# Gathers of a two-layer graph kernel: buffers awaited per group of four, indices copied three batches ahead

## The chip, the cores and the metric

One Trainium2 chip, one of its cores. The time is that of the device in microseconds (us), from start to end of the program; the kernel before took 14879.7 us (median of 3 runs, 14873.69 to 14883.93). TensorE, VectorE, ScalarE and GpSimd are called PE, DVE, ACT and POOL, as the profile does; SP is SyncE, which only issues DMAs here. Each engine has a sequencer that reads its instruction stream in order, carries out waits and register operations itself and hands the rest to the engine.

## The reference, cut to what matters

6250 nodes of 128 float32, 206250 edges sorted by destination, 64 edge types.

```python
# layer 0 (L0)
msg = edge_weight[:, None] * x[src];  agg = segment_sum(msg, dst, N)
x = layernorm(x + (relu((x + agg) @ W1 + b1) @ W2 + b2))
# layer 1: three hops over the same edges; head = src, tail = dst
agg = x
for _ in range(3):
    h, t = agg[head], agg[tail]
    att = sum((h @ q_w) * tanh(rel * t @ k_w), axis=1)      # rel = edge_emb[edge_type]
    w = softmax of att over the edges of one head
    agg = normalise(segment_sum(w[:, None] * rel * t, head) / count)
    out = out + agg + x
x = layernorm(x + out)
```

Both layers read one row of 512 bytes for every edge, from an address that the data give: `x[src]` in L0, `agg[tail]` in each hop.

## The kernel before, in words

Edges are laid out in tiles of 128 (one per partition), 1664 tiles in all, so that the edges of one tile belong to one section of 128 nodes. Four tiles make a group (`GROUP`), and there are 416 groups (`z.slot_groups`). L0 goes once over the groups, each of the three hops once more: 1664 turns over a group, and 6656 gathers of 128 rows (64 KB).

Every engine runs its own software pipeline over the groups. A step `s` with number `i` holds the engine's share of several groups: `s.live(3)` is the work on group `i - 3`. `pipeline` (L125, for the hops) runs the first steps written out, then a hardware loop with `unroll` steps in its body, then the last ones written out. `phases` (L146, for L0) does this in blocks of 32 steps: twice `unroll` steps written out, then a loop for the rest. L0 also carries the second sort of the edges (its own matmuls, one-hots and DMAs) in the same steps.

In a hop, the chain of one group is: SP loads its `rel`, `mask` and four `window` tiles; POOL gathers its four `tails` tiles; ACT copies `rel` to PSUM (L1857); DVE multiplies it with the gathered rows into `rt` (L1771) and counts `s_rt` up; PE transposes `rt` (L1833, "rtt"); ACT copies that out (L1853); PE multiplies with `k_w` (L1829, "kw"); ACT takes tanh of it (L1849, `right`); PE forms the attention (L1818); DVE masks it (L1759); ACT takes the exponential (L1866, `weight`); PE transposes it (L1825), ACT copies that out (L1846, `weight_t`), PE sums the messages (L1838, "acc"), and DVE adds them to the section's sums (L1753). A step of ACT has the order `weight_t`, `right`, (index copy), rtt, `rel`, `weight`, `fade`. So each group passes from PE to ACT or DVE five times, each time by a semaphore.

In L0, ACT multiplies the gathered rows with the edge weights (L1394) and counts `s_rt` up, and PE sums them with one-hot matrices (L1406).

The gathers are issued by `pool_rows` (L616), the same for L0 and the hops. It works in batches of two groups (`BATCH`, eight gathers). The ring of row buffers holds four groups (`RING`), that of indices two batches. For each batch in the loop POOL's sequencer waits (L632 to L634) until both groups that had the buffers are used up (`freed` counts `s_rt` by 2) and until the batch's indices are copied (`copied`), then hands over eight indirect DMAs, then does its register additions (L636, L637) and waits for the next. The indices are copied by ACT out of the edge table (`scalar_idx`, L645 and L649): in step `i`, for even `i`, after the rows of group `i - 1` are used up, it copies those of groups `i + 2` and `i + 3`. The first two batches (16 gathers) are handed over at the start of a stage.

Of the kernel before, what the change touches and what calls it, by code (L numbers as in the profile page):

```python
# [15 lines left out]
P = 128  # L16
# [4 lines left out]
RING = 4  # L21
BATCH = 2
# [144 lines left out]
def gnn_two_layers(nc, x, src, dst, edge_type, edge_weight, w1, b1, w2, b2, edge_emb, q_w, k_w, out):  # L167
# [3 lines left out]
    with top:  # L171
# [492 lines left out]
        with ExitStack() as ctx:  # L664
# [60 lines left out]
            others = tensor(ctx, "l0_others", [P, z.slot_tiles + BATCH * GROUP], I32)  # L725
# [302 lines left out]
            idx = tensor(inner, "l0_idx", [P, 2, BATCH * GROUP], I32)  # L1028
# [385 lines left out]
            with nc.Block() as block:  # L1414
# [10 lines left out]
                def _(e):  # L1425
                    first_idx(e, others, idx)
                    phases(e, "ga", scalar_l0, z.slot_groups, steps, (UNROLL, 16 * GROUP))

                @block.vector
                def _(e):  # L1430
# [4 lines left out]
                    phases(e, "gv", vector_l0, z.slot_groups, steps, (UNROLL, GROUP * UNROLL))  # L1435
# [3 lines left out]
                def _(e):  # L1439
                    phases(e, "gt", tensor_l0, z.slot_groups, steps, (UNROLL, GROUP * UNROLL))  # L1440
            inner.close()
            s_copy_idx.base += z.slot_groups // BATCH + 1
# [92 lines left out]
        others = tensor(top, "tails_of_slots", [P, z.slot_tiles + BATCH * GROUP], I32)  # L1535
# [160 lines left out]
        for hop in range(HOPS):  # L1696
            with ExitStack() as ctx:
                qt = tensor(ctx, f"qt{hop}", [P, z.NP])
                idx = tensor(ctx, f"idx{hop}", [P, 2, BATCH * GROUP], I32)
# [44 lines left out]
                def vector_hop(s):  # L1744
# [21 lines left out]
                    if s.live(1):  # L1766
                        g4, g8 = s.slot(1, UNROLL), s.slot(1, UNROLL)
# [184 lines left out]
                with nc.Block() as block:  # L1952
                    @block.sync
                    def _(e):
                        e.wait_ge(s_qt.h, s_qt.at(node_groups))
                        pipeline(e, f"hs{hop}", sync_hop, z.slot_groups, deep, (UNROLL,) if first else (UNROLL, GROUP * UNROLL))
# [14 lines left out]
                    def _(e):  # L1971
                        vector_q(e)
                        pipeline(e, f"hd{hop}", vector_hop, z.slot_groups, deep, (UNROLL, 2 * UNROLL, GROUP * UNROLL, 16 * GROUP, 32))
# [3 lines left out]
                    def _(e):  # L1977
                        tensor_q(e)
                        pipeline(e, f"he{hop}", tensor_hop, z.slot_groups, deep, (UNROLL, GROUP * UNROLL, 16 * GROUP))

                    @block.scalar
                    def _(e):
                        first_idx(e, others, idx)
                        scalar_q(e)
                        pipeline(e, f"ha{hop}", scalar_hop, z.slot_groups, deep, (UNROLL, GROUP * UNROLL, 32))
                        scalar_nodes(e)
                s_copy_idx.base += z.slot_groups // BATCH + 1
# [62 lines left out]
```

## Time and profile before

| | |
|---|---|
| median of 3 runs | 14879.7 us |
| span of the profiled execution, first to last instruction | 14895.7 us |
| the three runs' times | 14873.69, 14879.7, 14883.93 us |
| PE busy | 9009.4 us (60%) |
| DVE, ACT busy | 6224.1 us (42%), 6149.7 us (41%) |
| POOL busy | 6417.6 us (43%) |
| granted TensorE clock, mean | 0.725 |
| L0 (gathers from 160.5 to 3251.3 us) | 1664 gathers |
| hops (gathers from 3532.0 to 14810.8 us) | 4992 gathers |

The profiled execution has no time of its own beside its span; the span is 16 us above the median of the runs. "Busy" of POOL is the time in which descriptors of a gather were written, not the transfer. A row "[6.54 <-ACT idx L649]" says that the engine sat idle for 6.54 us before this instruction and that what ended the idle time was ACT's instruction of line 649; "issue" is time for which the profile shows no wait, "remote" a semaphore event that it can put down to no instruction that had just ended. POOLq and DVEq are the sequencers' own instructions. The starts of PE's rows are recorded, their ends are modelled.

### The profile page before, as it was taken

The numbers are of one execution on the slowest core, as the hardware profiler recorded it, in microseconds if no ns is written. First come the engines' busy times: TensorE is split into PE (matmuls) and PEld (weight loads), VectorE is DVE, ScalarE is ACT, GpSimd is POOL, SyncE is SP. The second block draws the span as 40 slices with busy tenths as digits, with TensorE's granted clock in tenths as the row PEclk, the third lists the DMA queues.
The fourth block names the chain that finished last, engine by engine and source line by source line (L and its number), as shares of the span: only waits on it lengthen the run. The fifth ranks groups of instructions, "written<-read, shape, count | busy, mean of one in ns | idle before, by whom it ended". The sixth has DMA issues, their size and how long they took to land. (4 is left out here: it accounts for less than half of the span.)

```text
span 14895.7 us, 251017 instructions
## 1 busy us (share of the span) xinstructions
PE 9009.4 (60%) x47197; PEld 6806.5 (46%) x47197; DVE 6224.1 (42%) x27880; ACT 6149.7 (41%) x15788; POOL 6417.6 (43%) x6756
## 2 busy tenths in 40 slices
PE   2465555566777777777755555555555556555665
PEld 2343443444555555555544444444444444444444
DVE  3555555565333333333343333333334333333334
ACT  1355555553333333333334444444443444444443
POOL 4554554442444434444334444444434444444443
PEclk7566666667777777777777777777777777777777
DMA  2111111112444444444433333333343333333333
GB/s 63 37 37 34 36 35 35 33 35 77 127 125 126 125 125 126 125 125 126 124 102 105 106 104 106 104 105 101 108 99 105 104 104 107 102 105 105 109 109 93
DMA packets 1390477, 1399.81 MB, mean 94 GB/s; under 512 B 239512, under 2 KB 1066681, under 8 KB 1390137
## 3 DMA queue, kind: packets, MB, share of 16 engines
q1 hardware_dynamic: 1173398, 951.42, 21.2%
q0 software_dynamic: 216064, 444.28, 12.3%
q10 hardware_dynamic: 876, 2.56, 0.1%
q8 instruction: 51, 0.84, 0.0%
q14 instruction: 88, 0.71, 0.0%
HBM read 888.87 MB, written 183.76 MB: 72 GB/s over the span
## 5 line engine op out<-in xcount | busy, mean ns | idle before, releaser
L621 POOL DMA_INDIRECT tails<-node_rows,idx x4992 | 4732.3, 948 | 6564.6 <-ACT idx L649 5017.2
L1753 DVE SCALAR_TENSOR_TENSOR acc<-acc,fade,banks 128x129 f32 x4992 | 1718.4, 344 | 5486.8 <-remote 3164.9
L1838 PE MATMUL banks<-rt,weight_t 128*128 128x129 f32 x9984 | 1783.3, 335 | 1486.3 <-issue 802.1
L1838 PEld LDWEIGHTS banks<-rt,weight_t 128*128 128x128 f32 x9984 | 1607.8, 244 | 1631.4 <-issue 1206.6
L621 POOL DMA_INDIRECT l_rows<-in_x_dram,l_idx x1664 | 1585.1, 953 | 1529.5 <-ACT l_idx L649 1017.3
L1846 ACT ACTIVATE weight_t<-banks 128x512 f32<-128x512 f32 x1248 | 745.5, 597 | 3569.1 <-remote 2286.4
L1825 PE MATMUL banks<-ident,weight 128*128 128x128 f32 x4992 | 1070.4, 353 | 1878.0 <-ACT weight L1866 1767.1
L1818 PE MATMUL banks<-right,window 128*128 128x128 f32 x9984 | 1774.8, 335 | 459.9 <-issue 459.2
L1818 PEld LDWEIGHTS banks<-right,window 128*128 128x128 f32 x9984 | 1590.2, 242 | 538.2 <-issue 510.7
L1829 PE MATMUL banks<-rtt,k_sb 128*128 128x512 f32 x2496 | 1741.3, 789 | 1.4 <-ACT rtt L1853 1.4
L1825 PEld LDWEIGHTS banks<-ident,weight 128*128 128x128 f32 x4992 | 752.0, 181 | 2041.5 <-ACT weight L1866 1931.4
L1759 DVE CUSTOM_DVE_ANT_0 att<-banks,mask 128x128 f32<-128x128 f32 x4992 | 1236.7, 285 | 888.7 <-remote 574.4
L1866 ACT ACTIVATE weight<-att,low 128x128 f32<-128x128 f32 x4992 | 1583.4, 395 | 1.7 <-DVE low L1789 1.5
L1853 ACT ACTIVATE rtt<-banks 128x512 f32<-128x512 f32 x1248 | 743.4, 596 | 1597.2 <-remote 1447.3
L1849 ACT ACTIVATE right<-banks 128x512 f32<-128x512 f32 x1248 | 744.4, 596 | 1535.2 <-remote 798.3
L1833 PEld LDWEIGHTS banks<-ident,rt 128*128 128x128 f32 x4992 | 781.9, 172 | 1247.7 <-issue 894.1
L1771 DVE TENSOR_TENSOR rt<-banks,tails 128x512 f32<-128x512 f32 x1248 | 857.9, 687 | 547.2 <-remote 180.2
L1833 PE MATMUL banks<-ident,rt 128*128 128x128 f32 x4992 | 937.3, 321 | 241.5 <-DVE rt L1771 237.0
L1239 ACT ACTIVATE apart<-spread,spot_left 128x256 f32<-128x256 f32 x1534 | 655.2, 495 | 1030.0 <-remote 761.9
L1406 PE MATMUL banks<-l_weighed,l_hot 128*128 128x128 f32 x3328 | 756.5, 395 | 428.2 <-DVE acc L1371 217.7
L1406 PEld LDWEIGHTS banks<-l_weighed,l_hot 128*128 128x128 f32 x3328 | 649.6, 289 | 559.2 <-issue 549.1
L1394 ACT ACTIVATE l_weighed<-l_rows,l_weights 128x128 f32<-128x128 f32 x1664 | 526.8, 387 | 546.1 <-remote 394.4
(309 smaller groups left out, 9792.2 us busy)
## 6 DMA issues: line engine op xcount, KB each, us to landing
window<-qt SPq DMA_DIRECT2D x4992, 64.0 KB
rel<-rel_kept SPq DMA_DIRECT2D x832, 256.0 KB
rows_in<-tile_rows SPq DMA_DIRECT2D x416, 256.0 KB
rel_kept<-rel SPq DMA_DIRECT2D x416, 256.0 KB
mask<-mask_kept SPq DMA_DIRECT2D x832, 128.0 KB
tails<-node_rows,idx POOLq DMA_INDIRECT x4992
mask_kept<-mask SPq DMA_DIRECT2D x416, 128.0 KB
l_rows<-in_x_dram,l_idx POOLq DMA_INDIRECT x1664
```

The lines of the kernel that those rows point to most:

```text
L621: e.indirect_dma_start(out=rows[:, g, t % GROUP, :], out_offset=None, in_=of, in_offset=bass.IndirectOffsetOnAxis(ap=idx[:, b, t:t + 1], a ...
L1406: mm = s.e.matmul(bank[g2][:, t * P:t * P + P], hot[:, g2, t, :], weighed[:, g2, t, :], start=True, stop=True)
L1753: e.scalar_tensor_tensor(to, to, fade[:, g2, t:t + 1], bank[b_acc + t // 2][:, t % 2 * WIDE:t % 2 * WIDE + WIDE], ALU.mult, ALU.add).then_ ...
L1759: e.tensor_tensor_reduce(att[:, g2, t, :], bank[b_att][:, t * P:t * P + P], mask[:, g4, t, :], 1.0, START, ALU.add, ALU.min, tile_low[:, g ...
L1771: e.tensor_tensor(rt[:, g4, :, 0:z.D], of, tails[:, g8, :, :], ALU.mult).then_inc(s_rt.h, 1)
L1818: mm = e.matmul(bank[b_att][:, t * P:t * P + P], window[:, g4, t, :], right[:, g2, t * P:t * P + P], start=True, stop=True)
L1825: mm = e.transpose(bank[b_et][:, t * P:t * P + P], weight[:, g2, t, :], ident[:, :])
L1829: e.matmul(bank[b_kw][:, :], k_sb[:, :], rtt[:, s.slot(2, 2), :], start=True, stop=True).then_inc(s_kw.h, 1)
L1833: mm = e.transpose(bank[b_rtt][:, t * P:t * P + P], rt[:, s.slot(1, UNROLL), t, 0:z.D], ident[:, :])
L1838: mm = e.matmul(bank[b_acc + t // 2][:, t % 2 * WIDE:t % 2 * WIDE + WIDE], weight_t[:, s.slot(4, 2), t, :], rt[:, s.slot(4, UNROLL), t, :] ...
L1846: e.activation(weight_t[:, s.slot(4, 2), :, :].rearrange("p t d -> p (t d)"), bank[b_et][:, :], ACT.Copy).then_inc(s_ets.h, 1)
L1866: e.activation(weight[:, g2, t, :], att[:, g2, t, :], ACT.Exp, scale=-1.0, bias=low[:, g4, t + 1:t + 2]).then_inc(s_exp.h, 1)
```

## The change

The ring of row buffers keeps its four groups, but POOL now waits for each group by itself: before the four gathers of group g it waits until group g - 4 is used up, hands over four gathers, adds 1 to `freed`, and goes to the next group. The ring of indices grows from two batches to four (`HELD` = 8 groups). `first_idx` copies four batches ahead of the loop, and in step `i` ACT copies the indices of groups `i + 6` and `i + 7` where it copied those of `i + 2` and `i + 3`, with the same wait (group `i - 1` used up); POOL waits for a batch's indices once per two groups. The loops over the groups of all engines go over eight steps (`TURN`) where they went over four, with the rates of their counters doubled: in `pipeline` 51 turns a hop where there were 102, in `phases` 16 steps written out and two turns of eight where there were 8 and six of four.

```diff
+HELD = 8
+TURN = 8
@@ pool_rows
-            def batch(b):
-                for t in range(BATCH * GROUP):
-                    g = b * BATCH + t // GROUP
-                    e.indirect_dma_start(out=rows[:, g, t % GROUP, :], out_offset=None, in_=of,
-                                         in_offset=bass.IndirectOffsetOnAxis(ap=idx[:, b, t:t + 1], axis=0)).then_inc(sp_tail[g].h, 16)
-
-            for b in range(2):
-                e.wait_ge(s_copy_idx.h, s_copy_idx.at(b + 1))
-                batch(b)
+            def gather(g):
+                b, first = g // BATCH % (HELD // BATCH), g % BATCH * GROUP
+                for t in range(GROUP):
+                    e.indirect_dma_start(out=rows[:, g % RING, t, :], out_offset=None, in_=of,
+                                         in_offset=bass.IndirectOffsetOnAxis(ap=idx[:, b, first + t:first + t + 1], axis=0)).then_inc(sp_tail[g % RING].h, 16)
+
+            for g in range(RING):
+                if g % BATCH == 0:
+                    e.wait_ge(s_copy_idx.h, s_copy_idx.at(g // BATCH + 1))
+                gather(g)
...
-            e.reg_mov(freed, s_free.at(BATCH))
-            e.reg_mov(copied, s_copy_idx.at(3))
-            with e.Fori(0, z.slot_groups // BATCH // 2 - 1):
-                for b in range(2):
-                    e.wait_ge(s_free.h, s_free.at(BATCH))
-                    e.wait_ge(s_free.h, freed)
-                    e.wait_ge(s_copy_idx.h, copied)
-                    batch(b)
-                    e.reg_add(freed, freed, BATCH)
-                    e.reg_add(copied, copied, 1)
+            e.reg_mov(freed, s_free.at(1))
+            e.reg_mov(copied, s_copy_idx.at(RING // BATCH + 1))
+
+            def freed_gather(g):
+                e.wait_ge(s_free.h, s_free.at(1))
+                e.wait_ge(s_free.h, freed)
+                if g % BATCH == 0:
+                    e.wait_ge(s_copy_idx.h, copied)
+                gather(g)
+                e.reg_add(freed, freed, 1)
+                if g % BATCH == 0:
+                    e.reg_add(copied, copied, 1)
+
+            with e.Fori(0, z.slot_groups // HELD - 1):
+                for g in range(RING, RING + HELD):
+                    freed_gather(g)
+            for g in range(RING, HELD):
+                freed_gather(g)
@@ first_idx, scalar_idx
-            for b in range(2):
+            for b in range(HELD // BATCH):
...
-                s.e.activation(idx[:, (s.i // BATCH + 1) % 2, :], others[:, bass.ds(s.at(lambda i: GROUP * (i + BATCH)), BATCH * GROUP)], ACT.Copy)\
+                s.e.activation(idx[:, (s.i // BATCH - 1) % (HELD // BATCH), :], others[:, bass.ds(s.at(lambda i: GROUP * (i + HELD - BATCH)), BATCH * GROUP)], ACT.Copy)\
@@ the loops (one of seven)
-                        pipeline(e, f"he{hop}", tensor_hop, z.slot_groups, deep, (UNROLL, GROUP * UNROLL, 16 * GROUP))
+                        pipeline(e, f"he{hop}", tensor_hop, z.slot_groups, deep, (TURN, GROUP * TURN, 32 * GROUP), TURN)
```

## Rows read from the trace of the kernel before

**Rows 1.** The page, part 5 (line engine op, count, busy, mean ns, idle before, releaser).

```profile
L621 POOL DMA_INDIRECT tails<-node_rows,idx x4992 | 4732.3, 948 | 6564.6 <-ACT idx L649 5017.2
```

**Rows 2.** Busy time by stretch, instructions on the gathered rows alone (hops, then L0).

```profile
core 0: us, DVE busy (x) POOL busy (x), PEclk, DMA share, GB/s
4000.00:7000.00 3000.00, 219.15 (x318) 1218.66 (x1280) 0.74 0.42 125
8000.00:11000.00 3000.00, 234.61 (x342) 1291.94 (x1367) 0.75 0.37 105
11500.00:14500.00 3000.00, 236.97 (x345) 1307.12 (x1383) 0.76 0.38 106
...
300.00:3100.00 2800.00, 470.90 (x1488) 1423.47 (x1495) 0.64 0.14 36
```

**Rows 3.** Waits of hop 1, 8000 to 11000 us: total us, times, longest.

```profile
POOL tails L621 <- ACT idx L649: 1321.2, 171, 10.5
...
ACT rtt L1853 <- remote: 574.3, 124, 7.4
```

**Rows 4.** Timeline of POOL in hop 1: a run of eight, the next run's first.

```profile
9025.32 0.95 POOL L621 DMA_INDIRECT tails<-node_rows,idx  x1 [6.54 <-ACT idx L649]
...
9034.07 0.94 POOL L621 DMA_INDIRECT tails<-node_rows,idx  x1 [0.30 <-issue]
9043.84 0.95 POOL L621 DMA_INDIRECT tails<-node_rows,idx  x1 [8.82 <-ACT idx L649]
```

**Rows 5.** Timeline of ACT in hop 1, over two groups.

```profile
9037.18 0.60 ACT L1853 ACTIVATE rtt<-banks 128x512 f32<-128x512 f32 x1 [1.02 <-remote]
...
9042.86 0.20 ACT L649 ACTIVATE idx<-tails_of_slots 128x8 int32 x1
9043.22 0.60 ACT L1853 ACTIVATE rtt<-banks 128x512 f32<-128x512 f32 x1 [0.16 <-PE banks L1833]
...
9050.33 0.60 ACT L1849 ACTIVATE right<-banks 128x512 f32<-128x512 f32 x1 [2.27 <-issue]
9055.41 0.60 ACT L1853 ACTIVATE rtt<-banks 128x512 f32<-128x512 f32 x1 [4.48 <-remote]
```

**Rows 6.** Timeline of DVE and of PE in the same two groups.

```profile
9038.30 0.69 DVE L1771 TENSOR_TENSOR rt<-banks,tails 128x512 f32<-128x512 f32 x1 [0.58 <-ACT banks L1857]
...
9047.17 0.60 PE L1833 MATMUL banks<-ident,rt 128*128 128x128 f32 x4
```

**Rows 7.** POOL's sequencer behind a run: of eight (9000 to 9045), of sixteen.

```profile
L636 POOLq FUSED_REGOPS  x2: 43/47/51, 9012.0 to 9028.3; - x2
...
L628 POOLq MOVE  x1: 38/38/38, 3538.5 to 3538.5; - x1
```

**Rows 8.** Timeline at the start of hop 0: first and last of sixteen gathers, ACT.

```profile
3531.97 0.95 POOL L621 DMA_INDIRECT tails<-node_rows,idx  x1 [17.11 <-ACT idx L643]
...
3550.72 0.94 POOL L621 DMA_INDIRECT tails<-node_rows,idx  x1 [0.30 <-issue]
...
3538.81 0.60 ACT L1893 ACTIVATE turned<-banks 128x512 f32<-128x512 f32 x1 [0.70 <-PE banks L1883]
3541.88 0.60 ACT L1893 ACTIVATE turned<-banks 128x512 f32<-128x512 f32 x1 [2.47 <-PE banks L1876]
...
3553.23 0.60 ACT L1893 ACTIVATE turned<-banks 128x512 f32<-128x512 f32 x1 [6.49 <-remote]
```

**Rows 9.** Timeline of ACT in L0.

```profile
506.17 1.28 ACT L1394 ACTIVATE l_weighed<-l_rows,l_weights 128x128 f32<-128x128 f32 x4 [9.20 <-PE banks L1406]
...
507.82 1.27 ACT L1394 ACTIVATE l_weighed<-l_rows,l_weights 128x128 f32<-128x128 f32 x4
```

**Rows 10.** DVE in hop 1, 8000 to 11000 us: all busy instructions; its sequencer's.

```profile
8000.00:11000.00 3000.00, 1756.42 (x8897) 1372.92 (x8897) 1082.59 (x5814) 1222.89 (x3250) 1291.94 (x1367) 0.75 0.37 105
...
L108 DVEq ALU_OP  x1710: 40/40/40, 8003.7 to 10997.0; - x190
L108 DVEq FUSED_REGOPS  x1368: 8/46/726, 8002.8 to 10997.7; - x196
L135 DVEq COMPARE_BRANCH  x85: 56/56/721, 8029.0 to 10978.2; - x85
```

**Rows 11.** The page, part 3: the queue that fetches instructions.

```profile
q14 instruction: 88, 0.71, 0.0%
```

More of the change, by code:

```diff
@@ L723, in _ @@
                         e.tensor_tensor(pay[:, 1, :], type_at[:, :], lower[:, :], ALU.add)
-            others = tensor(ctx, "l0_others", [P, z.slot_tiles + BATCH * GROUP], I32)
+            others = tensor(ctx, "l0_others", [P, z.slot_tiles + (HELD - BATCH) * GROUP], I32)
             weights = tensor(ctx, "l0_weights", [P, z.slot_tiles])
@@ L1027, in gnn_two_layers @@
             inner = ExitStack()
-            idx = tensor(inner, "l0_idx", [P, 2, BATCH * GROUP], I32)
+            idx = tensor(inner, "l0_idx", [P, HELD // BATCH, BATCH * GROUP], I32)
             rows = tensor(inner, "l0_rows", [P, RING, GROUP, z.D])
@@ L1426, in _ @@
                     first_idx(e, others, idx)
-                    phases(e, "ga", scalar_l0, z.slot_groups, steps, (UNROLL, 16 * GROUP))
+                    phases(e, "ga", scalar_l0, z.slot_groups, steps, (TURN, 32 * GROUP), TURN)
                 @block.vector
@@ L1434, in _ @@
                     e.wait_ge(s_column.h, 1)
-                    phases(e, "gv", vector_l0, z.slot_groups, steps, (UNROLL, GROUP * UNROLL))
+                    phases(e, "gv", vector_l0, z.slot_groups, steps, (TURN, GROUP * TURN), TURN)
                     e.wait_ge(s_taken.h, z.slot_tiles)
@@ L1439, in _ @@
                 def _(e):
-                    phases(e, "gt", tensor_l0, z.slot_groups, steps, (UNROLL, GROUP * UNROLL))
+                    phases(e, "gt", tensor_l0, z.slot_groups, steps, (TURN, GROUP * TURN), TURN)
             inner.close()
-            s_copy_idx.base += z.slot_groups // BATCH + 1
+            s_copy_idx.base += (z.slot_groups + HELD) // BATCH - 1
             for s in (s_rt, s_acc):
@@ L1532, in gnn_two_layers @@
             s_stored.base += 48
-        others = tensor(top, "tails_of_slots", [P, z.slot_tiles + BATCH * GROUP], I32)
+        others = tensor(top, "tails_of_slots", [P, z.slot_tiles + (HELD - BATCH) * GROUP], I32)
         parted = tensor(top, "parted", [P, z.slot_tiles])
@@ L1698, in gnn_two_layers @@
                 qt = tensor(ctx, f"qt{hop}", [P, z.NP])
-                idx = tensor(ctx, f"idx{hop}", [P, 2, BATCH * GROUP], I32)
+                idx = tensor(ctx, f"idx{hop}", [P, HELD // BATCH, BATCH * GROUP], I32)
                 tails = tensor(ctx, f"tails{hop}", [P, RING, GROUP, z.D])
@@ L1766, in vector_hop @@
                     if s.live(1):
-                        g4, g8 = s.slot(1, UNROLL), s.slot(1, UNROLL)
+                        g4, g8 = s.slot(1, UNROLL), s.slot(1, RING)
                         here = (s_rel if first else s_copied, done(1))
@@ L1955, in _ @@
                         e.wait_ge(s_qt.h, s_qt.at(node_groups))
-                        pipeline(e, f"hs{hop}", sync_hop, z.slot_groups, deep, (UNROLL,) if first else (UNROLL, GROUP * UNROLL))
+                        pipeline(e, f"hs{hop}", sync_hop, z.slot_groups, deep, (TURN,) if first else (TURN, GROUP * TURN), TURN)
                         if first:
@@ L1972, in _ @@
                         vector_q(e)
-                        pipeline(e, f"hd{hop}", vector_hop, z.slot_groups, deep, (UNROLL, 2 * UNROLL, GROUP * UNROLL, 16 * GROUP, 32))
+                        pipeline(e, f"hd{hop}", vector_hop, z.slot_groups, deep, (TURN, 2 * TURN, GROUP * TURN, 16 * GROUP, 32 * GROUP), TURN)
                         vector_nodes(e)
@@ L1984, in _ @@
                         scalar_q(e)
-                        pipeline(e, f"ha{hop}", scalar_hop, z.slot_groups, deep, (UNROLL, GROUP * UNROLL, 32))
+                        pipeline(e, f"ha{hop}", scalar_hop, z.slot_groups, deep, (TURN, GROUP * TURN, 64), TURN)
                         scalar_nodes(e)
-                s_copy_idx.base += z.slot_groups // BATCH + 1
+                s_copy_idx.base += (z.slot_groups + HELD) // BATCH - 1
                 for s in (s_oht, s_rel, s_copied) if first else (s_copied,):
```

## The prediction

> **What bounds the kernel now.** I read the busy shares first, then the stages, the waits, and then timelines. No engine is full: PE is busiest with 60% of the span, POOL has 43%. So the bound is a chain, and it has to be found in one cycle of a hop. The stages first: a group takes four gathers, so the three hops take 3000/(1280/4) = 9.38, 3000/(1367/4) = 8.78 and 3000/(1383/4) = 8.68 us a group, 8.95 on average, and L0 2800/(1495/4) = 7.49 [rows 2]. A gather occupies POOL for 0.95 us [rows 1] and is followed by the next after 1.25 us: eight start from 9025.32 to 9034.07 [rows 4]. Four make 5.0 us, so POOL could serve a group in 5.0 us where it takes 9. It sits idle for 6.5 to 8.8 us before a run [rows 4], nearly always until ACT's index copy; over hop 1 that is 1321 of 3000 us in 171 waits [rows 3]. That looks like the bound which this change takes away. It isn't the whole of it: the other engines stand still too, and not for want of rows.
>
> In rows 5 ACT's copy rtt comes once per group. From 9037.18 to 9043.22 a group takes 6.04 us, while POOL is idle. From 9043.22 to 9055.41 it takes 12.19 us, and that is the group beside which POOL's run goes (the run that begins at 9043.84 [rows 4]). What ACT waits for at 9055.41 is a transposition whose four matmuls PE's record has at 9047.17, over by 9047.77 [rows 6]; the result is passed on 7.6 us later, and the profile calls it "remote": no instruction had just ended. All of this happens while gathers run, and not during all of their time. Call the stretch in which PE's results are passed on late a hold. It begins about when POOL's sequencer has handed over the last gather of a run and goes to its next wait: 2.98 us into the run of eight that begins at 9025.32 the register addition stands (9028.3 [rows 7]). At the start of a hop sixteen gathers go in one piece from 3531.97, the sequencer is through at 3538.5 (6.5 us in, 0.41 us a gather) [rows 7], and ACT still gets PE's results with 0.70 us of waiting at 3538.81, 6.8 us in; the next come after 2.47 and later after 6.49 us [rows 8]. So the onset follows the sequencer (3.0 us for eight, 6.5 for sixteen), not the transfers. The hold ends after the last gather: 9037.18 - 9034.07 = 3.1 us after its start [rows 4, 5], 3553.23 - 3550.72 = 2.5 us in the run of sixteen [rows 8]; I take 2.9. A run of eight thus has a hold from 3.0 to 8.75 + 2.9 = 11.65 us, 8.65 us long. While POOL's sequencer waits after that, nothing is late: the group of 6.04 us lies there.
>
> Two groups cost 6.04 + 12.19 = 18.23 us, of which 8.65 are hold, and two free groups would be 12.08. So a hold costs 6.15 us net, and 2.5 us of work still get through it. Not the want of rows bounds a hop, but a free group, plus the hold.
>
> **The change, part by part.** *The wait per group* is the part that decides. The first gather of a group can be handed over when `rt` of the group four earlier is done. Before, the run waited for the index copy, at 9042.86, 4.56 us after `rt` began (9038.30) [rows 5, 6]; this delay goes. What is late next is the next hold, which now begins earlier in the cycle and once per group. Counted from ACT's rtt at the end of a hold (0): `rt` starts at 9038.30 - 9037.18 = 1.12 and takes 0.69 [rows 5, 6]; from the copy's end at 9043.06 to the first gather are 0.78 us [rows 4, 5], and I take the same for the wait on `s_rt`; so the first gather starts at 2.59. Four gathers are handed over in 4 x 0.37 = 1.5 us (2.98/8 each), so the hold begins at 4.1. The last of them starts 3 x 1.25 = 3.75 after the first, and the hold ends 2.9 later, at 9.24. Its length is 5.15 us, two of them 10.3 where one of 8.65 stood: each run pays its 2.9 us tail. Of the free group's 6.04 us, 4.1 are done before the hold begins; 1.94 are left (`right`, then rtt). In the run of rows 5, `right` passes within the hold at 9050.33 and rtt comes only when it ends, so I let rtt again come at the end: a cycle of 9.24 us a group.
>
> The price from both sides. If at the end of the hold `rt` could start at once (0.3 us) without ACT's rtt and `rel` copy, the cycle would be 0.3 + 0.69 + 0.78 + 3.75 + 2.9 = 8.4. If the work that passes through a hold is in proportion to its length (2.5 x 5.15/8.65 = 1.5), the cycle is 5.15 + 6.04 - 1.5 = 9.7. I take 9.24, as rtt at the end is what row 9055.41 shows. Three hops: (9.24 - 8.95) x 1248 groups = +360 us, between -680 and +940.
>
> In *L0* the cycle starts at ACT's weighing (1.28 us [rows 9]), so the first gather starts 1.28 + 0.78 = 2.06 after the hold. With one group per hold it is 2.06 + 3.75 + 2.9 = 8.7 us. But there two weighings can follow one another (506.17 and 507.82 [rows 9]), then POOL's second wait is met while it hands over the first four, and eight go in one run as before: (2.06 + 8.75 + 2.9)/2 = 6.9 us a group. Now it is 7.49. I take the middle, 7.8: +0.3 x 416 = +130 us, between -245 and +500.
>
> *Indices three batches ahead.* The same ACT instruction (0.20 us) in the same place, with the same wait; only POOL no longer waits for it. Two more copies at each of four starts, 8 x 0.2 = 1.6 us, beside POOL's first gathers: nothing. With the copy out of the way, POOL waits on `s_rt` alone; queued behind that wait are only gathers, and only `rt` or the weighing wait for those. As four groups are always ahead, that slack is three groups, some 27 us, and no row shows an engine waiting for landed rows in the hops. So earlier gathers bring nothing by themselves.
>
> *Loops over eight.* Half the branches go: hop 1 has 85 on DVE in 3000 us [rows 10], so some 102 per hop become 51. A branch with its register work takes some 0.3 us of a sequencer that has mostly waited at that point; 153 x 0.3 = 46 us at most, 0 at least; I take -20. A DVE body grows: busy and register instructions alone are (5814 + 1710 + 1368)/342 = 26 a step [rows 2, 10], so over 104 a turn become over 208. Whether they must be fetched again each turn no row of a loop this long shows; now the whole program has 88 fetches of 8 KB on that queue [rows 11]. At worst each of 153 turns waits for two fetches, each no longer than the 2.9 us from a gather to its landing: +890; at best, behind DVE's waits for holds, 0. I take 0: waits of over 5 us stand in each cycle. The Trainium skill (Runtime: NRT & Kernel Launch, Instruction fetch mechanics) says that most engines keep two blocks of 16 KiB, 256 instructions each, and that a branch to a block outside stalls; by that rule a DVE body of waits and loads included, well over 208, may lie over three blocks and be fetched in every turn, and the sum would go towards its upper end. The row has pieces of 8 KB, not 16.
>
> Sum: +360 + 130 - 20 = +470 on the span of 14895.7, thus 15366; the median of the runs lies 16 us below the span, so 15350 us, 3.2% slower.
>
> **Rivals.** *A, short holds let the work through (faster).* The place is the PE handover of rtt (L1833 to L1853), the price the part of a hold that work is lost in. A short hold may end before anything has queued up; for it speaks that 2.5 us pass even through a long one and that some copies come 1 or 2 us before its end (rtt at 9037.18 waited only 1.02 us). With three cycles in four at 8.4 and the rest at 9.24, the hops take 8.6: -430; L0 at 7.0 -205; 14240 us. It decides as soon as a cycle is under 8.95 us, i.e. if ACT's rtt comes over 0.3 us before the hold's end. *B, work through a hold is in proportion (much slower).* 9.7 us in the hops, +940, and L0 at 8.7, +500: 16320. Against it: the first copy in a hold is little late. *C, the doubled bodies are fetched again* in DVE's hops and a third of the +890 shows: 15650. *D, the change doesn't do what it says:* `rt` of two groups come so close that POOL's runs stay eight long, and the cycle stays as it is. In the hops `rt` is 6 to 12 us apart and four gathers are handed over in 1.5 us, so this holds for L0 at most: 14880.
>
> **How the numbers follow.** The forecast has 0.45 (its own range 15050 to 15700), A 0.27, B 0.12, C 0.09, D 0.07. Of the forecast and D together 0.08 lie within 0.2% (30 us), which is what a measurement of this kernel tells from no change; slower is 0.44 + 0.12 + 0.09 = 0.65, faster 0.27. The range reaches to A's time and leaves out the upper part of B: 14250 to 16000.
>
> **What would show it.** Right: runs of four gathers in the hops, 5 us long and 9.2 us apart; idle time before them released by DVE `rt`, not by ACT idx; every group with a late rtt ("remote") where now every second has one; between two rtt of ACT never the 6.04 us of a free group. Wrong: handovers that are late before the sequencer is through with a run, or not late with runs of four; rtt copies that stand well before the hold's end (then A); a DVE idle time at each loop turn (then C). The prediction is wrong as a whole if the hold isn't tied to POOL's wait behind a running gather.

## The result, and the profile after

The changed kernel took 13615.14 us (median of 4 runs, 13612.1 to 13628.3) beside 14881.82 us for the kernel before (14873.69 to 14899.28): a ratio of 0.9156, interval 0.9142 to 0.917, 8.4% faster. The forecast was 15350 us, with a range from 14250 to 16000. The sign was wrong and the time lies below the range.

The page of the changed kernel: parts 1 and 3, and the row of part 5 that answers to [rows 1].

```profile
span 13610.3 us, 246443 instructions
PE 8336.0 (61%) x47197; PEld 6331.7 (47%) x47197; DVE 6182.0 (45%) x27880; ACT 6100.7 (45%) x15796; POOL 6431.7 (47%) x6756
...
q14 instruction: 424, 3.47, 0.1%
...
L623 POOL DMA_INDIRECT tails<-node_rows,idx x4992 | 4751.2, 952 | 5446.5 <-DVE rt L1782 3995.5
```

The gathers (L623 now) no longer wait for ACT's index copy but for `rt`, as forecast, and idle 5446 us where it was 6565. Busy time by stretch, on the gathered rows alone, answering to [rows 2]; the columns are those:

```profile
3400.00:6400.00 3000.00, 275.44 (x399) 1537.66 (x1596) 0.88 0.52 157
6600.00:10000.00 3400.00, 272.09 (x398) 1509.77 (x1597) 0.80 0.37 108
10200.00:13500.00 3300.00, 276.25 (x404) 1527.94 (x1616) 0.81 0.39 112
...
300.00:2900.00 2600.00, 465.77 (x1472) 1405.70 (x1476) 0.65 0.14 38
```

| us per group | before [rows 2] | after | forecast | difference x 416 |
|---|---|---|---|---|
| hop 0 | 9.38 | 3000/(1596/4) = 7.52 | 9.24 | -774 |
| hop 1 | 8.78 | 3400/(1597/4) = 8.52 | 9.24 | -108 |
| hop 2 | 8.68 | 3300/(1616/4) = 8.17 | 9.24 | -212 |
| L0 | 7.49 | 2600/(1476/4) = 7.05 | 7.8 | -183 |

The sum is -1277 us; the spans differ by 14895.7 - 13610.3 = 1285. Three fifths of the gain are in hop 0, where the granted clock is 0.88 now and was 0.74.

The timeline of hop 0 shows the cycle: POOL, then PE, DVE and ACT in the same stretch. "Hold" is the prediction's word for the stretch in which PE's results are passed on late.

```profile
5503.39 0.95 POOL L623 DMA_INDIRECT tails<-node_rows,idx  x1 [3.11 <-DVE rt L1782]
...
5507.15 0.95 POOL L623 DMA_INDIRECT tails<-node_rows,idx  x1 [0.30 <-issue]
5510.84 0.94 POOL L623 DMA_INDIRECT tails<-node_rows,idx  x1 [2.74 <-DVE rt L1782]
```

```profile
5506.50 0.23 PE L1823 MATMUL banks<-emb_lo,hot_type 64*128 64x128 bf16 x1
```

```profile
5509.40 0.69 DVE L1782 TENSOR_TENSOR rt<-banks,tails 128x512 f32<-128x512 f32 x1 [3.09 <-remote]
```

```profile
5503.40 0.60 ACT L1864 ACTIVATE rtt<-banks 128x512 f32<-128x512 f32 x1 [0.36 <-PE banks L1844]
...
5509.55 0.60 ACT L1857 ACTIVATE weight_t<-banks 128x512 f32<-128x512 f32 x1 [3.46 <-PE banks L1836]
...
5511.40 0.59 ACT L1864 ACTIVATE rtt<-banks 128x512 f32<-128x512 f32 x1
```

Four gathers start within 3.76 us. 2.25 us after the last one's start `rt` starts, after a "remote" wait: the hold has ended. It takes 0.69 us, and 0.75 us after its end the next run starts: 3.76 + 2.25 + 0.69 + 0.75 = 7.45 us. ACT's rtt comes after the next run's first gather (5511.40 against 5510.84), no longer before it.

In hop 0 `rt` doesn't wait for a copy of `rel` by ACT, as the kernel in words has it: only hops 1 and 2 copy `rel`, in hop 0 PE makes it (L1823). That product was over at 5506.73, 2.67 us before `rt` started. The cycle above stands for its hop: over the 355 runs of four that begin between 3500 and 6400 us the medians of the four parts are 3.76, 2.22, 0.69 and 0.74, and 7.49 us from run to run. The packets of a run's last gather (queue q0, software_dynamic) end 2.18 us after its start (median, same stretch), so `rt` starts about when the last rows have been moved.

In hops 1 and 2 there are runs of four and of eight: 102 and 133 in the stretch of hop 1, 128 and 123 in that of hop 2. A run of four takes 7.7 us there until the next begins, one of eight 17.3 (medians), 8.65 a group. POOL's timeline in hop 1:

```profile
8006.63 0.95 POOL L623 DMA_INDIRECT tails<-node_rows,idx  x1 [7.61 <-DVE rt L1782]
...
8014.33 0.94 POOL L623 DMA_INDIRECT tails<-node_rows,idx  x1 [3.01 <-DVE rt L1782]
...
8023.07 0.95 POOL L623 DMA_INDIRECT tails<-node_rows,idx  x1 [0.30 <-issue]
8031.62 0.95 POOL L623 DMA_INDIRECT tails<-node_rows,idx  x1 [7.60 <-DVE rt L1782]
```

Three groups take 8031.62 - 8006.63 = 24.99 us, 8.33 each. When the second `rt` comes before a run's four gathers are over, the next four follow without a gap (0.30 us) and the hold is as long as before (ACT's `weight_t` at 8026.09 waited 9.34 us). Behind a run of four `rt` comes with the end of the hold here too: it starts 2.5 us after the last gather (median of the 230). In the run that begins at 8006.63 ACT's copy of `rel` was over at 8010.72, and `rt` (8012.91) stood behind DVE's update of the sums, which waited for PE until 8012.64. The waits of hop 1, answering to [rows 3]:

```profile
POOL tails L623 <- DVE rt L1782: 1456.6, 252, 10.7
ACT weight_t L1857 <- remote: 1383.6, 163, 9.6
```

### The profile page after: what moved, and what is told of

Its sections match the earlier page's. It is cut to its first block and busy times, and to the rows that moved or that the text cites. A ratio compares the mean times of both kernels' runs of the same rounds, so it can differ in the third digit from the quotient of the medians.

```text
span 13610.3 us, 246443 instructions
## 1 busy us (share of the span) xinstructions
PE 8336.0 (61%) x47197; PEld 6331.7 (47%) x47197; DVE 6182.0 (45%) x27880; ACT 6100.7 (45%) x15796; POOL 6431.7 (47%) x6756
## 5 line engine op out<-in xcount | busy, mean ns | idle before, releaser
L623 POOL DMA_INDIRECT tails<-node_rows,idx x4992 | 4751.2, 952 | 5446.5 <-DVE rt L1782 3995.5
L1849 PE MATMUL banks<-rt,weight_t 128*128 128x129 f32 x9984 | 1701.7, 323 | 2772.7 <-DVE acc L1764 2367.7
L1849 PEld LDWEIGHTS banks<-rt,weight_t 128*128 128x128 f32 x9984 | 1474.6, 226 | 2985.6 <-issue 2105.4
L623 POOL DMA_INDIRECT l_rows<-in_x_dram,l_idx x1664 | 1584.4, 952 | 1343.9 <-ACT l_weighed L1405 831.9
L1840 PE MATMUL banks<-rtt,k_sb 128*128 128x512 f32 x2496 | 1456.8, 669 | 1.4 <-issue 1.4
L1844 PEld LDWEIGHTS banks<-ident,rt 128*128 128x128 f32 x4992 | 613.8, 147 | 1550.6 <-DVE rt L1782 1092.7
L1844 PE MATMUL banks<-ident,rt 128*128 128x128 f32 x4992 | 803.0, 285 | 618.7 <-DVE rt L1782 616.7
L1836 PE MATMUL banks<-ident,weight 128*128 128x128 f32 x4992 | 932.3, 319 | 205.1 <-issue 103.4
L1836 PEld LDWEIGHTS banks<-ident,weight 128*128 128x128 f32 x4992 | 724.5, 168 | 260.1 <-ACT weight L1877 174.6
```

What stands on the lines that cost most here:

```text
L623: e.indirect_dma_start(out=rows[:, g % RING, t, :], out_offset=None, in_=of, in_offset=bass.IndirectOffsetOnAxis(ap=idx[:, b, first + t:fi ...
L1836: mm = e.transpose(bank[b_et][:, t * P:t * P + P], weight[:, g2, t, :], ident[:, :])
L1840: e.matmul(bank[b_kw][:, :], k_sb[:, :], rtt[:, s.slot(2, 2), :], start=True, stop=True).then_inc(s_kw.h, 1)
L1844: mm = e.transpose(bank[b_rtt][:, t * P:t * P + P], rt[:, s.slot(1, UNROLL), t, 0:z.D], ident[:, :])
L1849: mm = e.matmul(bank[b_acc + t // 2][:, t % 2 * WIDE:t % 2 * WIDE + WIDE], weight_t[:, s.slot(4, 2), t, :], rt[:, s.slot(4, UNROLL), t, :] ...
```

## The experiments

Eighteen runs of fourteen kernels, in six groups that each shared a chip; the fourth and the sixth group had the same one, so there were five chips. The chips differ more than the kernels do. The kernel before took 14721.96 us beside the first four kernels, 9167.27 and 9168.81 us beside two groups of four, and 14746.38, 14894.46 and 14688.98 us beside the last three pairs. I call the first kind of chip one with holds, the second one without. Whether it is the chip or a condition that it was in at the time isn't shown. Ratios are to the kernel before on the same chip. The first four forecasts are in us and were made from the 14881.82 us of the first comparison; the chip of the first four runs was 1.1% faster.

### Which part of the change gives the gain (chip with holds)

**loops8**: the kernel before with only the loops over eight.

```diff
+TURN = 8
-  pipeline(e, f"hd{hop}", vector_hop, ..., (UNROLL, 2 * UNROLL, GROUP * UNROLL, 16 * GROUP, 32))
+  pipeline(e, f"hd{hop}", vector_hop, ..., (TURN, 2 * TURN, GROUP * TURN, 16 * GROUP, 32 * GROUP), TURN)
```

> The kernel before with only its loops over eight steps instead of four. Theory H (the gain is made by POOL's wait per group: runs of four gathers make holds short enough that PE doesn't idle and keeps its 2.4 GHz): no gain, 14850 to 15050 us (at most 46 us fewer branches, up to 170 us for each hop whose DVE body is fetched again each turn). Rival L (the loops bring it): near 13650 us.

Measured: 14663.35 us, 0.9972 (0.9955 to 0.999): the loops don't bring the gain.

**runs_of_eight**: the change, but POOL waits for two groups at once; indices still ahead.

```diff
-                e.wait_ge(s_free.h, s_free.at(1)); e.wait_ge(s_free.h, freed)
                 if g % BATCH == 0:
+                    e.wait_ge(s_free.h, s_free.at(BATCH)); e.wait_ge(s_free.h, freed)
                     e.wait_ge(s_copy_idx.h, copied)
```

> The kernel after, but POOL waits for two groups at once and hands over eight gathers in one run as before; indices stay three batches ahead. Theory H: holds are 8.65 us long again, TensorE's clock falls back to about 0.73, time 14400 to 14900 us. Rival I (the gain is that POOL no longer waits for ACT's index copy and starts some 4 us earlier): 13500 to 13800 us, as the whole change.

Measured: 14881.73 us, 1.011 (1.0084 to 1.0136). With runs of eight the gain is gone. Indices ahead with runs of eight are even 1.4% slower than loops8 on the same chip, most of it in hop 0 (3000/(1243/4) = 9.65 us a group against 3600/(1563/4) = 9.21); why is not shown.

**loops4**: the change with the loops of PE, DVE and SP left at four.

```diff
-  pipeline(e, f"he{hop}", tensor_hop, ..., (TURN, GROUP * TURN, 32 * GROUP), TURN)
+  pipeline(e, f"he{hop}", tensor_hop, ..., (UNROLL, GROUP * UNROLL, 16 * GROUP))
```

> The kernel after, with the loops of PE, DVE and SP over four steps again (ACT keeps eight, its index slot needs it). Theory H: hop 1 loses the refetches of DVE's body (some 3.4 us x 51 turns), 13400 to 13600 us. Rival L: 14500 us or more.

Measured: 13300.71 us, 0.9038 (0.9019 to 0.9058). Hop 1 of loops4, where the changed kernel has 8.52 us a group (same columns as above):

```profile
6600.00:9700.00 3100.00, 265.87 (x389) 1474.23 (x1559) 0.82 0.40 115
```

3100/(1559/4) = 7.95 us. The queue that fetches instructions, 6900 to 9900 us (hop 1) of the changed kernel; for 10200 to 13200 (hop 2) the same row has 8 packets:

```profile
q14 instruction: 220, 1.80, 0.2%
```

In hop 1 the loops of eight are fetched again, 220 pieces in 3000 us, five in each turn of eight groups (8 x 8.52 = 68 us). loops4 is faster than its forecast in us (13400 to 13600), and (8.52 - 7.95) x 416 = 237 us of hop 1 are at most what the fetches cost in the changed kernel. It can be much less: hop 2, with no such fetches, differs by 8.17 - 8.01 = 0.16 us a group too, and the whole of hop 1 has more runs of eight in the changed kernel than in loops4 (137 against 118). And no other trace shows a price. loops8 has 221 such pieces in 3000 us of hop 1 and takes 3000/(1408/4) = 8.52 us a group there, less than the 8.78 of the kernel before without them; late_release, below, has 241 in 2900 us and takes 7.51 us in hop 1 and 7.50 in hop 2. The Trainium skill (Runtime: NRT & Kernel Launch, Instruction fetch mechanics) states a stall for a branch to a block outside the two that are kept; the fetches agree with that in hop 1 and not in hop 2, and a stall can't be told from the time of the groups.

**late_release**: the change, but in the hops POOL waits for the tanh of group g - 4 instead of its `rt`.

```diff
-                        pool_rows(e, f"hop{hop}", tails, idx, node_rows, s_rt)
+                        pool_rows(e, f"hop{hop}", tails, idx, node_rows, s_th)
```

> The kernel after, but in the hops POOL waits for the tanh of the group four earlier (s_th) instead of its product rt, some 3 to 5 us later; runs stay four long. Theory H: the holds keep their length, only their place in the cycle moves: 13300 to 14000 us. Rival I: most of the gain goes, 14400 us or more.

Measured: 13052.75 us, 0.8878 (0.8853 to 0.8903), below both forecasts. The later start is not itself the gain. In hop 0, where nearly all runs are of four in both kernels, a group takes 3000/(1538/4) = 7.80 us against 7.52 in the changed kernel. The gain is in hops 1 and 2, 7.51 and 7.50 against 8.52 and 8.17, where each hop has 59 runs of eight and the changed kernel 137 and 123: with the wait for the tanh two runs of four join less often. So what the change gives is neither the indices ahead alone (runs_of_eight) nor the loops (loops8) nor the earlier start, but the run's length. The wait per group without the indices ahead was not run, so whether it needs them isn't shown.

### The chips without holds

**after_again** is the changed kernel, **late_loops4** joins loops4 and late_release, **late_again** repeats it; **spin12** has an empty loop of 12 turns (0.218 us each) on POOL's sequencer behind each four gathers, spin6 one of six; late_l0 releases late in L0 too; spin12_again repeats spin12.

```diff
                 gather(g)
+                with e.Fori(0, 12):
+                    e.reg_add(spun, spun, 1)
                 e.reg_add(freed, freed, 1)
```

> The changed kernel itself, beside the kernel before on this chip. Two conditions of the chip have been met: one with holds (PE's results passed on late while gathers run; the kernel before takes 14720 to 14880 us) and one without (the kernel before takes 9167 us, a group in the hops 5.0 us, the gathers back to back). Theory (the change gains only by shortening what a hold covers): with holds a ratio of 0.91 to 0.93 as at first; without holds POOL's gathers are the bound in both kernels, so 0.996 to 1.001. Rival (the indices copied ahead, or the loops over eight, give something by themselves): without holds still at least 1% faster, 0.99 or less. Second rival (refetched loops of eight, +3.4 us a turn in hop 1, cost the same everywhere): without holds 51 x 3.4 = 173 us slower, 1.02.

> The kernel after with both edits that helped: POOL waits for the tanh of the group four earlier in the hops, and the loops of PE, DVE and SP go over four. If their gains add (4% and 1.3 to 2%): 12750 to 12900 us. If the late release only shifted the phase of the refetches: 13050 us.

> The kernel after; behind each four gathers POOL's sequencer runs an empty loop of 12 turns (about 4 us of register work and branches) before it goes to its wait. Theory H1 (a hold is POOL's sequencer sitting in a semaphore wait while gathers run): no late handovers while it loops, hops at 6.5 to 7 us a group, 12000 to 12800 us. Rival T (the gathers' own descriptor writing and transfers make the hold, whatever the sequencer does): PE's results are late as before, 13300 us or more.

Measured, on two chips without holds: after_again 9143.68 us, 0.9971 (0.9961 to 0.9981); late_loops4 0.999, late_again 0.9988, late_l0 0.9989; spin12 0.9971, spin6 0.9971, spin12_again 0.9976. All within 0.3% of before, as the theory had it for a chip without holds; a gain of 1% from the indices or the loops, and a loss of 2% from the fetches, are both out. The forecasts for a chip with holds are not tested by these runs. after_again, stretch 7000 to 9000 us on the gathered rows, and POOL's timeline in hop 0:

```profile
7000.00:9000.00 2000.00, 276.95 (x402) 1512.09 (x1602) 1.00 0.66 185
```

```profile
5506.68 0.94 POOL L623 DMA_INDIRECT tails<-node_rows,idx  x1 [0.30 <-DVE rt L1782]
5507.92 0.94 POOL L623 DMA_INDIRECT tails<-node_rows,idx  x1 [0.30 <-issue]
```

2000/(1602/4) = 4.99 us a group: gather follows gather at 1.25 us without end, at the full granted clock, and nothing is late. Hop 1 has 225 fetched pieces from 5000 to 6800 us and takes the same 4.99 us. The change is worth 8.4% on a chip with holds and 0.3% on one without. SP's sequencer tells the two apart as well; its rows L110, 7000 to 7500 us, in the first profile of the changed kernel and in after_again (ns: least, median, most):

```profile
L110 SPq ALU_OP  x59: 5/41/726, 7001.3 to 7492.4; - x59
```

```profile
L110 SPq ALU_OP  x99: 37/37/43, 7017.1 to 7499.6; - x99
```

### Is it POOL's wait that makes a hold?

**before_spin40**: the kernel before, with 40 turns (8.7 us) on POOL's sequencer behind each run of eight, so that it stands in no wait through the hold. It ran on a chip without holds, then as **before_spin40_b** on one with them.

```diff
                     batch(b)
+                    with e.Fori(0, 40):
+                        e.reg_add(spun, spun, 1)
                     e.reg_add(freed, freed, BATCH)
```

> The kernel before with an empty loop of 40 turns (8.7 us) on POOL's sequencer behind each run of eight gathers, so that the sequencer is busy from 3.0 us to 11.7 us after the run's first gather, the whole of the stretch in which results came late. Theory 1 (a hold needs the sequencer standing in a wait): no holds in the hops, two groups take 12 to 13 us where they took 18.4, and the time is 0.70 to 0.80 of the kernel before's with holds. Theory 2 (the gathers' own traffic): 0.98 to 1.02 with holds; the turns themselves may take longer than 0.218 us inside a hold. Without holds both say slower, since a run of eight then comes every 10 us and the sequencer is not free for 11.7: two groups take about 12 us, 1.15 to 1.2 of the kernel before's 9167 us.

> The kernel before with the empty loop of 40 turns (8.7 us) on POOL's sequencer behind each run of eight gathers, once more, for a chip with holds. Theory 1: no holds in the hops, 0.70 to 0.80 of before (near 11200 us, what the same kernel took on a chip without holds, if holds are gone altogether). Theory 2: 0.98 to 1.02 of before. Without holds 1.22 again, which tells nothing.

Measured: 11197.2 us, 1.2214 (1.219 to 1.2239) without holds; 14954.78 us, one run, 14954.78/14746.38 = 1.014 with holds. The turns' additions on POOL's sequencer, 4000 to 6000 us, before_spin40 and then before_spin40_b:

```profile
L638 POOLq ALU_OP  x6170: 32/32/32, 4000.1 to 5999.9; - x200
```

```profile
L638 POOLq ALU_OP  x4332: 3/32/1397, 4000.3 to 6000.0; - x197
```

The sequencer is busy and the hold comes all the same: it even catches POOL's own register operations (up to 1.4 us for one of 0.03), and in hop 0 of before_spin40_b (4000 to 7500 us) a third of PE's results are copied by ACT over 0.5 us late, in before_spin40 none. The prediction's cause has fallen. Without holds the kernel took a little more than the 1.15 to 1.2 forecast. The ratio of 1.014 itself says little, since the stretched turns set the cycle: a run began at 9013.82 and the next at 9031.26, 17.4 us, most of it turns, and `rt` now waited for its rows, so that in hop 1 only 7% of PE's results fall into a hold:

```profile
DVE rt L1776 <- DMA tails<-node_rows,idx: 1186.4, 210, 10.2
```

**spin12_third**: spin12 on the same chip with holds.

> The changed kernel with the empty loop of 12 turns (2.6 us) on POOL's sequencer behind each four gathers, once more, for a chip with holds (kernel before near 14700 to 14900 us). Theory 1 (a hold needs POOL's sequencer standing in a wait while gathers run): 0.88 or less of the changed kernel's 0.9156 of before, so 0.81 or less of before. Theory 2 (a hold comes from the gathers' own traffic): 0.91 to 0.95 of before. Without holds 0.997 of before again, which tells nothing.

Measured: 12342.94 us, one run, 12342.94/14746.38 = 0.837, between the two forecasts. Its hop 1, with 241 fetches in the stretch:

```profile
6500.00:9200.00 2700.00, 265.21 (x385) 1442.89 (x1531) 0.88 0.47 131
```

2700/(1531/4) = 7.05 us a group against 8.52 in the changed kernel (another chip). POOL's timeline shows why:

```profile
8006.21 0.94 POOL L623 DMA_INDIRECT tails<-node_rows,idx  x1 [0.30 <-issue]
8009.35 0.94 POOL L623 DMA_INDIRECT tails<-node_rows,idx  x1 [2.19 <-issue]
...
8013.09 0.95 POOL L623 DMA_INDIRECT tails<-node_rows,idx  x1 [0.30 <-issue]
8016.20 0.94 POOL L623 DMA_INDIRECT tails<-node_rows,idx  x1 [2.16 <-issue]
```

Nearly all runs are four long now (two of eight in hop 0, one in hop 1, two in hop 2): the turns keep two of them from joining and leave a gap of 2.2 us, in which the held results pass. In hop 0, where the changed kernel has runs of four already, the turns give nothing: 2800/(1496/4) = 7.49 us against 7.52.

**spin_loops4**: spin12 with loops over four. 

> The changed kernel with loops over four on PE, DVE and SP and with the empty loop of twelve turns behind each four gathers. spin12 took 0.837 of before with its 222 refetched blocks in hop 1 still there and that hop at 7.05 us a group, as the others (7.47, 6.98). If the refetches are hidden beside runs of four: 0.837 again, within 0.5%. If they still cost something: 51 turns x up to 3.4 us = 173 us, 0.825. Without holds: 0.997 to 0.999.

Measured: 12567.68 us, 0.8433 (0.8404 to 0.8463), on another chip than spin12_third. It lies just above both forecasts (0.837 within 0.5%, and 0.825). No gain from taking the fetches away; against a single run on another chip that is all it says.

### What length of run, and what gap

**paced4** cuts the loop in four: four turns behind each gather of the changed kernel; **before_paced4** does the same in the kernel before, which still waits for two groups at once; **paced6** has six turns in the changed kernel.

The same lines stand in all three, with 6 for 4 in paced6:

```diff
                     e.indirect_dma_start(...).then_inc(...)
+                    with e.Fori(0, 4):
+                        e.reg_add(spun, spun, 1)
```

> The changed kernel with the empty loop cut in four: four turns (0.87 us) behind each gather instead of twelve behind four, so that POOL's sequencer hands a gather over about every 1.3 us, as fast as the engine works them off, and none stands queued. The kernel before with its sequencer kept busy through the hold took 1.014 of before, with register operations of POOL's own sequencer up to 1.41 us long: it isn't the wait that makes a hold. Theory 3 (a hold begins when the last gather of a run has been handed over and lasts while handed-over gathers run): with pacing the last is handed over 3.9 us into a run of 5 us, a hold covers 2 us instead of 5, a group takes 5.5 to 6.5 us in the hops, and the time is 0.70 to 0.78 of before (with holds; spin12 gave 0.837). Theory 4 (a hold goes with gathers running at all, whatever the sequencer does; the first 1.6 us of a run only seemed free): no better than spin12, 0.83 to 0.92. Without holds: 0.997.

> The kernel before, its two groups still awaited together, with the empty loop of four turns (0.87 us) behind each gather of a run of eight: the sequencer hands the last gather over about 9.1 us into the run instead of 3.0. Theory 3 (a hold begins when a run's last gather has been handed over): the hold covers 2.5 us instead of 8.65 of each two groups, which take some 12 to 14 us where they took 18.4; 0.68 to 0.78 of before. Theory 4 (a hold goes with gathers running, whatever has been handed over): results are late from about the start of the run on, the run is no shorter, 0.98 to 1.06 of before. Without holds: about 1.03, since four turns and the hand-over take 1.3 us where a gather takes 1.25.

> The changed kernel with six turns (1.3 us) behind each gather, 1.75 us from one to the next, so that the gathers of a group spread over 7 us, as long as a group took with four turns (7.1 us, 0.8216 of before). Theory 4 says that the stretch with a gather running then covers everything: the group takes at least 4 x 1.75 = 7.0 us for the hand-over alone, and as nothing is left between runs in which results come in time, 7.2 to 8.5 us, 0.83 to 0.95 of before. Theory 3 has no holds left at all and gives 7.0 to 7.1 us, 0.81 to 0.82. Without holds: four times 1.75 us are more than the 5.0 us of a group, 1.25 to 1.3.

Measured: paced4 12244.2 us, 0.8216 (0.8186 to 0.8247); before_paced4 12132.58 us, 0.8259 (0.8235 to 0.8283); paced6 12651.77 us, 0.8612 (0.8587 to 0.8637). The first stood just outside one forecast's band (0.83 to 0.92), before_paced4 far from both (0.68 to 0.78, 0.98 to 1.06), paced6 in the second's (0.83 to 0.95), though not for its reason. POOL's timeline in before_paced4, then in paced6:

```profile
5509.72 0.95 POOL L621 DMA_INDIRECT tails<-node_rows,idx  x1 [0.35 <-issue]
5511.01 1.09 POOL L621 DMA_INDIRECT tails<-node_rows,idx  x1 [0.35 <-issue]
5512.41 0.95 POOL L621 DMA_INDIRECT tails<-node_rows,idx  x1 [0.30 <-issue]
5515.64 0.96 POOL L621 DMA_INDIRECT tails<-node_rows,idx  x1 [2.28 <-issue]
```

```profile
5500.99 0.95 POOL L623 DMA_INDIRECT tails<-node_rows,idx  x1 [0.78 <-issue]
5502.72 0.95 POOL L623 DMA_INDIRECT tails<-node_rows,idx  x1 [0.79 <-issue]
```

In before_paced4 the gathers start mostly in runs of three and four, although they are awaited by eight: the hold stretches the sequencer's own turns (up to 0.95 us each operation), the next gather comes late, and this gap lets the results pass. The kernel throttles itself. In paced6 a gap of 0.8 us stands behind every gather. From PE's and ACT's rows of the traces I took how long after PE's last matmul of a transposition or product ACT's copy of it starts (mean over a stretch, and the share over 0.5 us):

```
kernel               hop  stretch      mean late us   over 0.5 us
before               0    4000-7000    2.89           48%
before               1    8000-11000   2.13           42%
changed              0    3500-6400    0.61           43%
changed              1    6600-10000   2.98           47%
late_release         0    3500-6500    1.50           59%
before_spin40_b      0    4000-7500    1.27           33%
spin12_third         0    3500-6200    0.56           46%
before_paced4        0    3500-6000    0.46           24%
paced6               0    3700-6400    0.05            0%
paced6               1    6600-9500    0.09            4%
after_again          0    2700-4700    0.07            0%
```

With 0.8 us between gathers no result of PE's is late in hop 0, and few and little in hop 1 (at most 0.9 us). spin12_third on the same chip, with 0.3 us inside its runs of four, has 46% late. It isn't the rate of the gathers: paced6 takes 7.25 us a group in hop 0 (2000/(1103/4)), less than the changed kernel's 7.52. Something of the hold is left in paced6: from 3500 to 6400 us 231 of 4486 register operations and branches of SP take over 0.15 us, where after_again has none. The lateness is not the time either. In hop 1 of the changed kernel results are later on average than before, and a group still takes 0.26 us less; paced6 has none late and is slower than paced4.

What bounds paced6 is the pace: four gathers 1.75 us apart are 7.0 of its 7.2 us a group, and `rt` waits for rows there:

```profile
DVE rt L1788 <- DMA tails<-node_rows,idx: 694.8, 270, 6.0
```

So neither reading that I had left is right. On a chip with holds, a hold goes with gathers that follow each other with 0.3 us between them, whatever POOL's sequencer does, and it ends behind the run's last gather, 2.2 us after that one's start in the runs of four above. When it begins isn't fixed by this. Of PE's results that were ready 3 to 4 us into a run of eight in hop 0, all 223 were late in the kernel before (4000 to 7300 us) and 223 of 226 in loops8, but none of 222 in runs_of_eight, on the same chip as loops8, and none of 122 in before_spin40_b; in the last, none of the 522 that were ready up to 5.5 us into a run was late, and all 227 from 6.5 us on were. The sequencer stood in a wait from 3 us on in loops8 and in runs_of_eight alike, so the wait doesn't set the onset either. What in the chip a hold is, what sets its onset, and why two of the five chips of these experiments didn't have it, stays open. A pace between four and six turns was not tried, and paced4 was not run on a chip without holds, where a hand-over every 1.3 us would be slower than the 1.25 us of a gather.

## Why the prediction was wrong, point by point

- **The bound.** Right: hops are bound by a chain in which PE's results come late while gathers run, and not by want of rows. Wrong is its cause, a wait of POOL's sequencer; the prediction had named this as what would make it wrong as a whole. The onset after the hand-over of eight and of sixteen [rows 7, 8] was one reading of two places. before_spin40_b shows the hold without the wait; paced6 shows that with a gap of 0.8 us behind each gather PE's results come in time. The onset itself follows neither the sequencer nor a fixed time from the run's start.
- **The step that failed: the cycle of 9.24 us.** It was 1.12 (from rtt to `rt`) + 0.69 + 0.78 + 3.75 + 2.9. The rows of hop 0 above give 0 + 0.69 + 0.75 + 3.76 + 2.25 = 7.45. The first term isn't there: DVE's `rt` is itself what the hold kept back and goes first when it ends, where the prediction let it queue behind ACT's rtt and copy of `rel`, as in the one cycle of rows 5 and 6. Those rows are of hop 1; in hop 0 `rt` waits for PE's own `rel`, and in hops 1 and 2, behind a run of four, ACT's copy has long been made. The last term is 0.65 us shorter: 2.9 was taken from the copies of ACT behind a run of eight and one of sixteen. Together 1.77 of the 1.79 us. In hops 1 and 2 runs of four take 7.7 us for the same reasons (2.5 for the 2.9), and the groups in runs of eight 8.65.
- **"A hold costs 6.15 us net"** took 6.04 us for a free group as given. The upper bound of 9.7 us was built on it, and the group came out at 7.52. PE was busy 2164.33/(1280/4) = 6.8 us a group in hop 0 before at a granted clock of 0.74 and 2404.94/(1596/4) = 6.0 after at 0.88. So the work itself was slower beside long holds; which part of the gain comes by the clock no run separates.
- **The bound of 8.4 us** used the same 2.9 and so didn't reach what came. With 2.25 it would have been 7.8, and the lower end of the range below what was measured.
- **L0**: 7.05, at the lower end of 6.9 to 8.7; the middle was the wrong choice.
- **Rival A** (a short hold lets the work through) had the sign and the place; its 14240 us came from the term above. **D** holds for hops 1 and 2 in part: about half the runs are still eight long, which the prediction had confined to L0, and the gain there is 108 and 212 us against 774 in hop 0. Its reason against D, that `rt` are 6 to 12 us apart, was read off cycles with runs of eight; once a hold ends, two `rt` come closer. **C**: the bodies are fetched again in hop 1 alone, and that costs 237 us at most and perhaps nothing (forecast 0, and +890 at most over all hops; the 2.9 us a fetch in that bound was the tail of a hold, and no row gives the price of a fetch). **B** is out.
- **The index copies ahead** bring nothing by themselves, as forecast (runs_of_eight 1.011 with them, loops8 0.9972 without).

## What to carry to other kernels

When results are late only while another engine's DMAs run, measure the lateness against the gap between these DMAs before giving it a cause; one empty loop between them tells more than the place of a wait. A cycle is to be written down with what was kept back going first when the hold ends, not in the order in which one timeline showed it. When an edit is said to give a gain by a later or an earlier start, count first what else it changes: late_release gained by fewer joined runs. And a kernel's gain can belong to the chip, or to the condition it is in: the same edit was worth 8.4% and 0.3%.

## What the runs showed of the hardware that I had not expected

- The same program took 9167 us on two chips and 14689 to 14894 us on the three others of the experiments. On the latter, gathers back to back hold up PE's results, SP's register operations (up to 0.73 us for one of 0.04) and POOL's own (1.4 us for 0.03).
- Pauses between POOL's gathers make the kernel faster there: four empty turns behind each gather, in runs still awaited by eight, take the kernel before to 0.8259, more than the change does (0.9156), and the change on top of it (paced4, 0.8216) adds nothing that can be told across chips. Both beat both kernels on a chip with holds.
- Loops of nearly the same length are fetched anew in hop 1 (220 pieces in 3000 us) and not in hop 2 (8), and on a chip without holds hop 1, with 225 pieces in 1800 us, takes no longer a group than hop 2 (4.99 us both).
- On a chip with holds a hold is over about when the last rows have been moved: the packets of a run's last gather end 2.18 us after its start, and `rt` starts after 2.22 (medians of hop 0 of the changed kernel).
